# Fixed filters of an image stage on 64x64 tiles of TensorE, with the crossing rows in a packed edge operand

## The chip, the cores and the metric

One core of a Trainium2 chip runs the whole program; the other cores have no work. The metric is the device time of one execution in microseconds (us). The engines are named as in the profile: PE is TensorE's matmuls, PEld its weight loads, DVE is VectorE, ACT is ScalarE, POOL is GpSimd, and SP is SyncE, whose queue issues nearly all DMAs.

## The reference, cut to what matters

The input is `x` of shape (8, 32, 128, 128): images, channels, rows, columns. Four layers follow each other, each adding to `x` a function of the normalised `x`. The change touches the first layer only:

```
x = relu(batchnorm(conv3x3(normalise(x)) + bias))      # y below
grad_x = ifft2(fft2(y) * Fx); grad_y = ifft2(fft2(y) * Fy)          # circular 3x3 Sobel filters
second_xx, second_yy = the same filters again, on grad_x and grad_y
out = second_xx + second_yy + grad_x**2 + grad_y**2 - 2*grad_x*grad_y + y
```

The last line is one linear filter of 5x5 (second_xx + second_yy + y) plus the square of one linear filter of 3x3 (grad_x - grad_y), both circular in rows and columns. All numbers are float32.

## The kernel before, in words

The program has stages, one after the other: the first convolution (to about 260 us), the fixed filters (281 to 731 us, the place of the change), a second layer of small products per pixel (753 to 1680 us), a third and fourth layer (to about 2140 us), and an inverse transform that writes the output.

In the filter stage an image lies with its 128 rows on the 128 partitions and channels and columns along the free axis. A 5x5 circular filter is then five matrix products, one for each column shift `d`: a 128x128 circulant matrix `circ[:, d, :]`, which holds the filter's column along the rows, times the image shifted by `d` columns. The 3x3 filter takes three. A matmul has 512 columns, which is four channels of 128 columns. So an image is 8 groups of four channels, each with `filter5` (L680, five matmuls) and `filter3` (L688, three matmuls). Each float32 matmul shows as two records in the profile. `yp` is the image after batch norm and ReLU, with four wrapped columns in front; ACT makes it from `yt`, a quarter of the channels at a time (`relu`, L960).

`ps` has eight banks. `filter5` of group n writes bank n % 2, `filter3` writes bank 2 + n % 2. ACT squares the second into `sq` (`gradient`, L972). DVE then does for each group (`curvature`, L1367): add the 5x5 result to `xt`, the image of the residual path (L1373, counted by `c5_used`); add the square (L1376, after the semaphore `c3_sq`); take the statistics of the four channels (L1205). `filter5` of group n waits for `c5_used` of group n - 2 and `filter3` for `c3_sq` of group n - 2, so PE works on one bank while the others are read.

The statistics of image h - 1 become its group norm while the filters of image h run: two small products on PE (`group_means`, L627, and `group_vars`, L634), a root on ACT, and scale and shift on DVE (L1225 to L1232). ACT then normalises all 32 channels (L956) into `xn1` in two blocks of 16 instructions, between its work for the groups 1 and 2 and behind group 2, squares them (L982), and DVE sums over channels (L1396) behind the groups 4 and 5. ACT also makes `yp` of image h + 1, a quarter behind each odd group. POOL copies the edge columns (L1166, L1167).

The order of all engines is the order of the code; nothing is reordered by a scheduler. SP's queue does in round h: load the `yt` of image h + 2 (L467), store `xt` of image h - 1 (L472), wait for the normalised image and store it to `xcl` (L477), load `xt` of image h + 1 (L480), in the rounds 1 to 3 issue 36 small DMAs each that place constants of the second layer (`place_tap`, L401 and L403), in round 4 issue 32 loads for the second layer (L446, L455), and store the pixel norms (L498). Each waits its turn behind the ones ahead of it.

## Time and profile before

| what | value |
|---|---|
| median of 3 runs | 2391.45 us (2381.02 to 2391.6) |
| profiled execution, its own time | 2396.21 us |
| its span, first to last instruction | 2394.4 us |
| mean granted clock of TensorE | 0.904 of full speed |
| filter stage, first to last filter matmul | 281.5 to about 731.5 us |
| PE busy in the whole span | 1968.2 us (82%) |
| DVE, ACT, POOL busy | 1210.4, 1137.6, 185.8 us |
| DMA | 306.13 MB, mean 128 GB/s |

### The profile page before, as it was taken

The numbers are of one execution on the slowest core, as the hardware profiler recorded it, in microseconds if no ns is written. First come the engines' busy times: TensorE is split into PE (matmuls) and PEld (weight loads), VectorE is DVE, ScalarE is ACT, GpSimd is POOL, SyncE is SP. The second block draws the span as 40 slices with busy tenths as digits, with TensorE's granted clock in tenths as the row PEclk, the third lists the DMA queues.
The fourth block names the chain that finished last, engine by engine and source line by source line (L and its number), as shares of the span: only waits on it lengthen the run. The fifth ranks groups of instructions, "written<-read, shape, count | busy, mean of one in ns | idle before, by whom it ended". The sixth has DMA issues, their size and how long they took to land.

```text
span 2394.4 us, 85342 instructions
## 1 busy us (share of the span) xinstructions
PE 1968.2 (82%) x38916; PEld 1390.3 (58%) x38916; DVE 1210.4 (51%) x2300; ACT 1137.6 (48%) x1986; POOL 185.8 (8%) x131
## 2 busy tenths in 40 slices
PE   4777599999996989988998999985468888877765
PEld 2344344444444777777777877764465666545654
DVE  3455334444446555555555555541567666722444
ACT  0111336666655555555555555542457766641210
POOL 1000000000010000000000000001333333200000
PEclk9998799999998999999999999997669999976555
DMA  6765844669453444443444344445445452495897
GB/s 136 185 167 124 166 92 101 172 171 230 150 156 114 68 70 81 68 80 67 78 69 78 65 80 71 73 75 172 107 133 155 144 164 85 108 206 167 169 294 221
DMA packets 610284, 306.13 MB, mean 128 GB/s; under 512 B 418236, under 2 KB 586054, under 8 KB 602566
## 3 DMA queue, kind: packets, MB, share of 16 engines
q1 hardware_dynamic: 599376, 283.93, 51.5%
q10 hardware_dynamic: 10560, 16.93, 2.9%
q8 instruction: 295, 4.83, 0.9%
q14 instruction: 53, 0.43, 0.1%
HBM read 172.28 MB, written 128.54 MB: 126 GB/s over the span
## 4 chain that ended last, share of the span: by engine, by line
PE 65%; DVE 9%; ACT 7%; SPq 7%; DMA 7%; issue 5%; ACTq 0%; POOL 0%; DVEq 0%
PE ps L685 12%; PE ps L644 12%; PE ps L764 11%; PE ps L692 7%; PE ps L723 7%; PE ps L748 6%; SPq L455 5%; ACT arena L956 4%; DMA arena<-xcl 4%; PE ps L803 3%; DVE arena L1496 2%; ACT arena L1044 2%; PE ps L918 2%; DMA arena<-x_dram 1%; DVE arena L1418 1%
## 5 line engine op out<-in xcount | busy, mean ns | idle before, releaser
L1418 DVE TENSOR_TENSOR arena<-arena 128x1024 f32<-128x1024 f32 (+1 forms) x308 | 350.7, 1160 | 240.3 <-ACT arena L1036 239.5
L748 PE MATMUL ps<-arena 62*64 62x108 f32 x11008 | 338.6, 257 | 91.8 <-DMA arena<-xcl 59.2
L1036 ACT ACTIVATE arena<-ps 128x1024 f32<-128x1024 f32 (+1 forms) x308 | 297.3, 982 | 150.7 <-PE ps L723 150.4
L748 PEld LDWEIGHTS ps<-arena 62*64 62x64 f32 x11008 | 291.5, 134 | 131.6 <-issue 37.2
L723 PE MATMUL ps<-arena 63*64 63x128 f32 (+1 forms) x9504 | 326.4, 271 | 28.9 <-issue 14.9
L1044 ACT COPY arena<-ps 128x864 f32<-128x864 f32 x258 | 222.4, 880 | 265.7 <-PE ps L764 241.5
L956 ACT ACTIVATE arena<-arena,nmr,rstd 128x128 f32<-128x128 f32 x752 | 295.2, 512 | 31.5 <-DVE nmr L1232 31.5
L723 PEld LDWEIGHTS ps<-arena 63*64 63x64 f32 x9504 | 280.4, 135 | 36.1 <-issue 20.6
L685 PE MATMUL ps<-arena 128*128 128x512 f32 x640 | 289.1, 597 | 14.6 <-ACT arena L970 14.6
L764 PE MATMUL ps<-arena 64*64 64x384 f32 (+1 forms) x3168 | 264.7, 482 | 1.2 <-issue 1.2
L685 PEld LDWEIGHTS ps<-arena 128*128 128x128 f32 x640 | 120.8, 190 | 167.9 <-issue 167.9
L764 PEld LDWEIGHTS ps<-arena 64*64 64x64 f32 x3168 | 149.6, 136 | 91.7 <-issue 26.7
L644 PE MATMUL ps<-arena 32*32 32x512 f32 x4608 | 172.2, 649 | 36.6 <-issue 30.7
L644 PE MATMUL ps<-arena,w_conv 32*32 32x512 f32 x4608 | 176.5, 640 | 12.0 <-DVE arena L1531 6.7
L692 PE MATMUL ps<-arena 128*128 128x512 f32 x384 | 176.3, 594 | 0.0
L644 PEld LDWEIGHTS ps<-arena 32*32 32x32 f32 x4608 | 99.7, 107 | 102.6 <-issue 68.9
L1205 DVE BATCH_NORM_STATS2 st<-arena 128x6 f32<-128x128 f32 x768 | 156.2, 276 | 2.2
L1181 POOL TENSOR_TENSOR arena<-arena 128x1024 f32<-128x1024 f32 x32 | 83.4, 2639 | 937.7 <-DMA arena<-l_dram 937.3
L1431 DVE TENSOR_SCALAR arena<-ps,bias 128x192 f32<-128x192 f32 x172 | 60.0, 411 | 189.0 <-PE ps L764 189.0
L1376 DVE TENSOR_TENSOR arena<-arena 128x512 f32<-128x512 f32 x64 | 47.4, 740 | 160.5 <-ACT arena L975 159.7
L644 PEld LDWEIGHTS ps<-arena,w_conv 32*32 32x32 f32 x4608 | 78.6, 107 | 82.1 <-issue 52.9
L692 PEld LDWEIGHTS ps<-arena 128*128 128x128 f32 x384 | 72.0, 189 | 89.2 <-issue 87.7
(135 smaller groups left out, 1806.1 us busy)
## 6 DMA issues: line engine op xcount, KB each, us to landing
arena<-xcl SPq DMA_DIRECT2D x688, 60.0 KB, 2.7
x_dram<-arena SPq DMA_DIRECT2D x16, 2048.0 KB, 7.1
arena<-x_dram SPq DMA_DIRECT2D x16, 2048.0 KB, 15.1
arena<-l_dram SPq DMA_DIRECT2D x32, 1024.0 KB, 13.5
xcl<-arena SPq DMA_DIRECT2D x8, 3072.0 KB, 10.9
arena<-in_x SPq DMA_DIRECT2D x32, 512.0 KB, 10.5
y_dram<-arena ACTq DMA_DIRECT2D x64, 256.0 KB, 5.7
arena<-in_x SPq DMA_DIRECT2D x16, 1024.0 KB, 16.4
```

What stands on the lines that cost most here:

```text
L455: sp.dma_start(dst, src).then_inc(xs_loaded[e], 16)
L644: m = pe.matmul(ps[C * j:C * j + C, bank + g, :], weights[C * g:C * g + C, dy, dx, :], tile[C * g:C * g + C, r:r + CR, dx:dx + W], start=t ...
L685: m = pe.matmul(ps[:, n % 2, :], circ[:, d, :], yp[h % 2][:, 4 * n:4 * n + 4, 4 - d:4 - d + W], start=d == 0, stop=d == 4)
L692: m = pe.matmul(ps[:, 2 + n % 2, :], circ[:, 5 + d, :], yp[h % 2][:, 4 * n:4 * n + 4, 4 - d:4 - d + W], start=d == 0, stop=d == 2)
L723: mm = pe.matmul(ps[T2 * t:T2 * t + T2, fill_bank(f) + e, i:sub * n:sub], w_op[T2 * e:T2 * e + C + LANES + 1, FILL * f + sub * e + i, :], ...
L748: mm = pe.matmul(ps[T2 * j:T2 * j + T2, bank + t, STEPS * uu:STEPS * uu + STEPS], xs[T2 * t:T2 * t + C + LANES, e, j, u, :], own[T2 * t:T2 ...
L764: mm = pe.matmul(ps[T2 * t:T2 * t + T2, MIX_BANK + j, 0:n // 2 * HALF_U * PIX], w_mix[T2 * j:T2 * j + T2, kk, :], ysb[T2 * j:T2 * j + T2, ...
L956: m = nc.scalar.activation(tile[:, c], src[:, c], ACT.Identity, scale=rstd[:, gn.slot + n % 2, c:c + 1], bias=nmr[:, gn.slot + n % 2, c:c ...
L1036: nc.scalar.activation(own, raw_op, ACT.Tanh).then_inc(fill_tanh, 1)
L1044: nc.scalar.copy(ysb[:, :, e, u:u + UG, :].rearrange("p t u s -> p t (u s)"), ps[:, bank:bank + 2, 0:UG * STEPS]).then_inc(main_out_a, 1)
L1205: m = nc.vector.bn_stats(st[:, c, :], tile[:, c, :])
L1418: nc.vector.tensor_tensor(own, own, d, ALU.add).then_inc(op_done, 1)
```

## The change

Each filter's 128x128 product is cut into products of 64x64. Rows 0 to 63 and rows 64 to 127 of the image are two halves. Only the circulant's diagonal blocks are used, and the rows that cross from one half into the other (four at most) come from a separate operand.

- Each group is now a pair of groups: 8 channels, of which the even ones go to one bank and the odd ones to the next. For odd channels the two halves lie swapped in `yp`, so that the four combinations of row half and output half are four different tiles of the array. A column shift is four matmuls (two banks, two halves), 64 rows by 64 outputs by 512 columns.
- The crossing rows lie in `edge[k]`, for 16 channels each: the last four rows of the other half in five column shifts, 20 partitions for each half. They are copied out of `yp` by ten DMAs of 4 partitions x 2108 elements (`edges_in`). Two copies per image make 20 DMAs. `w_edge` holds the matching filter rows, placed once by 16 small DMAs. Each pair of groups takes four more matmuls for each filter, 20 rows by 64 outputs.
- Semaphores count pairs: `filter5` of pair p starts when `c5_used` shows both banks of the pair before as read, and `filter3` when `c3_sq` does.
- `yt` is gone: `y` is loaded straight into `yp`, which has three buffers, in four DMAs per image in place of two, and ReLU works in place.
- The taps are spread over the rounds 1 to 5 of SP, two each (one in the last), 24 small DMAs in place of 36.

```diff
@@ -55,6 +55,7 @@
+EDGE = C * YPW // 2
@@ -246,13 +247,14 @@
-        xt = [planes(0), planes(22656)]
-        yt = [planes(4096), planes(8192)]
-        yp = [planes(12288, YPW), planes(26752, YPW)]
...
+        xt = [planes(0), planes(22912)]
+        yp = [planes(4096, YPW), planes(8320, YPW), planes(27008, YPW)]
+        edge = [part(12544 + EDGE * n, EDGE).rearrange("p (c w) -> p c w", w=YPW) for n in range(2)]
...
+        w_edge = part(48076, 2 * T2).rearrange("p (a n) -> p a n", a=2)
@@ -432,9 +436,40 @@
-            rows_in(yt[0], image(y_dram, 0), yt_loaded[0])
-            rows_in(yt[1], image(y_dram, 1), yt_loaded[1])
+            def y_in(b):
+                own = yp[b % 3][:, :, YPW - W:YPW].rearrange("p (c s) w -> p c s w", s=2)
+                src = image(y_dram, b).rearrange("h (c s) w -> s h c w", s=2)
+                for s in range(2):
+                    for half in range(2):
+                        rows, at = slice(T2 * half, T2 * half + T2), T2 * ((half + s) % 2)
+                        sp.dma_start(own[rows, :, s], src[s, at:at + T2]).then_inc(y_loaded[b % 3], 16)
+            def edges_in(b, k):
+                sp.wait_ge(relu_done, 4 * b + 2 * k + 2)
+                if b:
+                    sp.wait_ge(c3_mm, 8 * (b - 1) + 4 * k + 4)
+                n = EDGE - 4
+                src = yp[b % 3][:, 16 * k:16 * k + 16, :].rearrange("p c w -> p (c w)")
+                dst = edge[k].rearrange("p c w -> p (c w)")
+                for half in range(2):
+                    last = T2 * (1 - half) + T2 - 4
+                    for d in range(5):
+                        sp.dma_start(dst[T2 * half + 4 * d:T2 * half + 4 * d + 4, 0:n], src[last:last + 4, 4 - d:4 - d + n]).then_inc(edge_loaded[k], 16)
+            y_in(0)
+            y_in(1)
             rows_in(xt[1], image(x, 1), xt_loaded[1])
+            sp.wait_ge(circ_made, 1)
+            sp.wait_ge(edge_clear, 1)
+            for half in range(2):
+                for d in range(8):
+                    at = T2 * half + 4 * (d % 5)
+                    sp.dma_start(w_edge[at:at + 4, d // 5, :], circ[T2 - 4:T2, d, T2:P]).then_inc(edge_made, 16)
+            for part_ in range(2):
+                edges_in(0, part_)
@@ -463,9 +498,12 @@
-                    sp.wait_ge(relu_done, 4 * (h + 1))
-                    rows_in(yt[h % 2], image(y_dram, h + 2), yt_loaded[h % 2])
+                    if h:
+                        sp.wait_ge(c3_mm, 8 * h)
+                    y_in(h + 2)
                 if h == 0:
+                    for part_ in range(2):
+                        edges_in(1, part_)
@@ -476,12 +514,14 @@
+                    edges_in(h + 1, 0)
+                if h + 1 < B:
                     sp.wait_ge(x1_stored[par], 16 * ((h - 1) // 2 + 1))
                     rows_in(xt[par], image(x, h + 1), xt_loaded[par])
-                if h <= 3:
+                if h <= 5:
                     if h == 1:
                         sp.wait_ge(op_taken, 16 * TAPS)
-                    for j in range(3 * (h - 1), 3 * h):
+                    for j in range(2 * (h - 1), min(2 * h, TAPS)):
@@ -496,6 +536,8 @@
+                if h + 1 < B:
+                    edges_in(h + 1, 1)
@@ -677,29 +719,43 @@
-            def filter5(h, n):
-                pe.wait_ge(relu_done, 4 * h + n // 2 + 1)
-                after(pe, c5_used, 8 * h + n - 1)
-                for d in range(5):
-                    m = pe.matmul(ps[:, n % 2, :], circ[:, d, :], yp[h % 2][:, 4 * n:4 * n + 4, 4 - d:4 - d + W], start=d == 0, stop=d == 4)
-                m.then_inc(c5_mm, 1)
-            def filter3(h, n):
-                after(pe, c3_sq, 8 * h + n - 1)
-                for d in range(3):
-                    m = pe.matmul(ps[:, 2 + n % 2, :], circ[:, 5 + d, :], yp[h % 2][:, 4 * n:4 * n + 4, 4 - d:4 - d + W], start=d == 0, stop=d == 2)
-                m.then_inc(c3_mm, 1)
+            def filters(h, p, kernel, first, shifts, bank):
+                for d in range(shifts):
+                    for s in range(2):
+                        for half in range(2):
+                            rows, to = slice(T2 * half, T2 * half + T2), T2 * ((half + s) % 2)
+                            pe.matmul(ps[to:to + T2, bank + s, :], circ[rows, first + d, rows],
+                                      yp[h % 3][rows, 8 * p + s:8 * p + 8:2, 4 - d:4 - d + W], start=d == 0, stop=False)
+                for s in range(2):
+                    for half in range(2):
+                        rows, to = slice(T2 * half, T2 * half + 20), T2 * ((half + s) % 2)
+                        c = 8 * (p % 2)
+                        m = pe.matmul(ps[to:to + T2, bank + s, :], w_edge[rows, kernel, :], edge[p // 2][rows, c + s:c + 8:2, 0:W], start=False, stop=True)
+                return m
+            def filter5(h, p):
+                pe.wait_ge(relu_done, 4 * h + p + 1)
+                if p % 2 == 0:
+                    pe.wait_ge(edge_loaded[p // 2], 160 * (h + 1))
+                after(pe, c5_used, 8 * h + 2 * p)
+                filters(h, p, 0, 0, 5, 0).then_inc(c5_mm, 2)
+            def filter3(h, p):
+                after(pe, c3_sq, 8 * h + 2 * p)
+                filters(h, p, 1, 5, 3, 2).then_inc(c3_mm, 2)
+            pe.wait_ge(edge_made, 16 * 16)
             for h in range(B):
-                for n in range(8):
-                    filter5(h, n)
-                    if n == 1 and h:
+                for p in range(4):
+                    filter5(h, p)
+                    if p == 0 and h:
+                        group_means(gn1, h - 1)
+                    filter3(h, p)
+                    if p == 0 and h:
                         group_vars(gn1, h - 1)
-                    filter3(h, n)
-                    if n == 0 and h:
-                        group_means(gn1, h - 1)
@@ -960,13 +1016,12 @@
-                    act.wait_ge(yt_loaded[h % 2], 32 * (h // 2 + 1))
-                    after(act, c3_mm, 8 * (h - 1))
+                    act.wait_ge(y_loaded[h % 3], 64 * (h // 3 + 1))
                 for c in range(QC * q, QC * q + QC):
-                    m = nc.scalar.activation(yp[h % 2][:, c, 4:YPW], yt[h % 2][:, c, :], ACT.Relu, scale=bn_a[:, c:c + 1], bias=bn_b[:, c:c + 1])
+                    m = nc.scalar.activation(yp[h % 3][:, c, 4:YPW], yp[h % 3][:, c, 4:YPW], ACT.Relu, scale=bn_a[:, c:c + 1], bias=bn_b[:, c:c + 1])
                 m.then_inc(relu_main, 1)
                 act.wait_ge(relu_main, 4 * h + q + 1)
-                tile = yp[h % 2][:, QC * q:QC * q + QC, :]
+                tile = yp[h % 3][:, QC * q:QC * q + QC, :]
@@ -1366,16 +1424,17 @@
-                own = xt[h % 2][:, 4 * n:4 * n + 4, :].rearrange("p c w -> p (c w)")
+                c0 = 8 * (n // 2) + n % 2
+                own = xt[h % 2][:, c0:c0 + 8 - n % 2:2, :]
                 if n == 0:
                     dve.wait_ge(xt_loaded[h % 2], 32 * (h // 2 + 1))
                 dve.wait_ge(c5_mm, 8 * h + n + 1)
-                nc.vector.tensor_tensor(own, own, ps[:, n % 2, :], ALU.add).then_inc(c5_used, 1)
+                nc.vector.tensor_tensor(own, own, ps[:, n % 2, :].rearrange("p (c w) -> p c w", c=4), ALU.add).then_inc(c5_used, 1)
                 dve.wait_ge(c3_sq, 8 * h + n + 1)
                 dve.wait_ge(c5_used, 8 * h + n + 1)
-                nc.vector.tensor_tensor(own, own, sq[:, n % 2, :], ALU.add).then_inc(c3_used, 1)
+                nc.vector.tensor_tensor(own, own, sq[:, n % 2, :].rearrange("p (c w) -> p c w", c=4), ALU.add).then_inc(c3_used, 1)
                 dve.wait_ge(c3_used, 8 * h + n + 1)
-                m = group_stats(xt[h % 2], 4 * n, 4)
+                m = group_stats(xt[h % 2], c0, 4, 2)
```

On PE, at the start of an image's filters, this stood before (L685 `filter5`, L692 `filter3`, L627 and L634 the two norm products; a row without waits follows the one with them):

```order
L627 MATMUL ps<-st,k 128x32 [waits gn1_stats]
L627 MATMUL ps<-st,k 128x32
L685 MATMUL ps<-arena 128x512 [waits c5_used,relu_done]
L685 MATMUL ps<-arena 128x512 x4
L634 MATMUL ps<-dev,k 128x32 [waits gn1_dev]
L634 MATMUL ps<-dev,k 128x32
L692 MATMUL ps<-arena 128x512 [waits c3_sq]
L692 MATMUL ps<-arena 128x512 x2
```

And this stands there now (L728 the shifts of either filter, L734 its edge products, L669 and L676 the two norm products):

```order
L728 MATMUL ps<-arena 64x512 [waits c5_used,edge_loaded0,relu_done]
L728 MATMUL ps<-arena 64x512 x19
L734 MATMUL ps<-arena 64x512 x4
L669 MATMUL ps<-st,k 128x32 [waits gn1_stats]
L669 MATMUL ps<-st,k 128x32
L728 MATMUL ps<-arena 64x512 [waits c3_sq]
L728 MATMUL ps<-arena 64x512 x11
L734 MATMUL ps<-arena 64x512 x4
L676 MATMUL ps<-dev,k 128x32 [waits gn1_dev]
L676 MATMUL ps<-dev,k 128x32
L728 MATMUL ps<-arena 64x512 [waits c5_used,relu_done]
```

Five and three matmuls for four channels became 24 and 16 for eight channels; a wait on `c5_used` now stands once per pair.

On SP, from round 4 into round 5, this stood before (L446 and L455 the second layer's loads, L498 the pixel norms, L360 loads of `y` or `x`, L472 the store of `xt`, L477 the store to `xcl`):

```order
L446 DMA arena<-nimg 30x4x32 x15
L455 DMA arena<-xcl 30x16x32 x16
L498 DMA nimg<-rn 128x192 [waits norm_root]
L360 DMA arena<-y_dram 64x32x128 [waits relu_done]
L360 DMA arena<-y_dram 64x32x128
L472 DMA x_dram<-arena 128x4096 [waits gn1_stats]
L477 DMA xcl<-arena 128x6144 [waits edge_done,gn1_out]
L360 DMA arena<-in_x 64x32x128 [waits x1_stored0]
```

And this stands there now (L460 the edge copies, L447 the loads of `y`, L364 of `x`):

```order
L481 DMA arena<-nimg 30x4x32 x15
L490 DMA arena<-xcl 30x16x32 x16
L538 DMA nimg<-rn 128x192 [waits norm_root]
L460 DMA arena<-arena 4x2108 [waits c3_mm,relu_done]
L460 DMA arena<-arena 4x2108 x9
L447 DMA arena<-y_dram 64x16x128 [waits c3_mm]
L447 DMA arena<-y_dram 64x16x128 x3
L510 DMA x_dram<-arena 128x4096 [waits gn1_stats]
L515 DMA xcl<-arena 128x6144 [waits edge_done,gn1_out]
L460 DMA arena<-arena 4x2108 [waits c3_mm,relu_done]
L460 DMA arena<-arena 4x2108 x9
L364 DMA arena<-in_x 64x32x128 [waits x1_stored0]
```

Ten edge copies stand behind the store to `xcl` and ahead of the load of `xt`, and ten more at the end of the round, behind everything that the round issues.

## Rows read from the trace of the kernel before

**Rows 1.** The chain that ended last, one line of code each: start us, us, what.

```profile
444.65 4.30 PE ps L685 x10
...
451.54 4.30 PE ps L685 x10
...
807.78 5.84 PE ps L764 x72
```

**Rows 2.** By windows: us; busy PE, PEld, DVE, ACT, POOL; clock, DMA share, GB/s.

```profile
458.80:514.80 56.00, 56.00 (x137) 25.02 (x137) 24.22 (x61) 34.61 (x85) 2.43 (x2) 1.00 0.67 171
```

**Rows 3.** Same stretch by lines: engine, op, names, shapes, count, busy us, mean ns, idle.

```profile
L956 ACT ACTIVATE arena<-arena,nmr,rstd 128x128 f32<-128x128 f32 x32 | 12.7, 576 | 0.0
...
L966 ACT ACTIVATE arena<-arena,bn_b,bn_a 128x128 f32<-128x128 f32 x32 | 12.7, 481 | 0.0
...
L1396 DVE TENSOR_REDUCE r<-arena 128x32 f32<-128x1024 f32 x4 | 4.7, 1204 | 0.0
...
L982 ACT ACTIVATE arena<-arena 128x1024 f32<-128x1024 f32 x4 | 4.1, 1052 | 2.9 <-DVE r L1396 2.8
```

**Rows 4.** Timeline of ACT and DVE inside that image: start us, us, line, op, names.

```profile
476.24 0.61 ACT L975 ACTIVATE arena<-ps 128x512 f32<-128x512 f32 x1
...
476.89 0.69 DVE L1376 TENSOR_TENSOR arena<-arena 128x512 f32<-128x512 f32 x1 [5.66 <-ACT arena L975]
...
477.61 0.87 DVE L1205 BATCH_NORM_STATS2 st<-arena 128x6 f32<-128x128 f32 x4
...
478.40 0.67 DVE L1373 TENSOR_TENSOR arena<-arena,ps 128x512 f32<-128x512 f32 x1
```

**Rows 5.** Timeline of DVE where the norm's scale is made.

```profile
463.57 0.19 DVE L1225 TENSOR_SCALAR sd<-ps 128x32 f32<-128x32 f32 x1 [1.26 <-PE ps L634]
...
464.55 0.68 DVE L1373 TENSOR_TENSOR arena<-arena,ps 128x512 f32<-128x512 f32 x1
```

**Rows 6.** Timeline of SP's queue ahead of the filters.

```profile
277.45 10.79 SPq L360 DMA_DIRECT2D arena<-in_x  x2
```

**Rows 7.** Windows over the first filter microseconds.

```profile
287.00:298.00 11.00, 11.00 (x26) 4.79 (x26) 2.94 (x7) 4.89 (x13) 0.00 (x0) 0.99 1.21 203
298.00:320.00 22.00, 22.00 (x52) 9.60 (x51) 7.16 (x19) 8.96 (x22) 0.00 (x0) 1.00 0.52 89
```

**Rows 8.** Timeline of PE at the first filters.

```profile
281.49 7.32 PE L685 MATMUL ps<-arena 128*128 128x512 f32 x10 [14.62 <-ACT arena L970]
```

**Rows 9.** Lines of small DMAs that SP issues: ns min, median, max to issue.

```profile
L424 SPq DMA_DIRECT2D arena<-in_conv_w x16: 427/502/594, 32.3 to 40.6; - x16
...
L401 SPq DMA_DIRECT2D w_dram<-op_dram x81: 712/713/5085, 383.5 to 527.6; - x81
```

**Rows 10.** Timeline of SP's queue in the fifth filter image.

```profile
555.32 12.25 SPq L446 DMA_DIRECT2D arena<-nimg  x16
567.61 8.12 SPq L455 DMA_DIRECT2D arena<-xcl  x16
```

**Rows 11.** Timeline of PE in the first convolution: the bracket is the idle time ahead.

```profile
62.34 4.45 PE L644 MATMUL ps<-arena 32*32 32x512 f32 x128 [1.85 <-issue]
...
132.29 7.03 PE L644 MATMUL ps<-arena 32*32 32x512 f32 x150 [2.84 <-issue]
```

**Rows 12.** Windows there, with the columns of Rows 2.

```profile
60.50:62.30 1.80, 0.00 (x0) 0.00 (x0) 0.57 (x1) 1.19 (x2) 0.00 (x0) 1.00 0.98 295
...
133.90:136.90 3.00, 3.00 (x66) 1.52 (x37) 1.51 (x3) 0.00 (x0) 0.00 (x0) 0.50 0.00 0
```

**Rows 13.** Timeline of PE where two tile shapes alternate.

```profile
1801.77 3.41 PE L644 MATMUL ps<-arena,w_conv 32*32 32x512 f32 x96
1805.10 2.00 PE L803 MATMUL ps<-k,arena 128*128 128x64 f32 x16
1807.03 3.41 PE L644 MATMUL ps<-arena,w_conv 32*32 32x512 f32 x96
```

**Rows 14.** By form: the spectrum's products.

```profile
L885 PE MATMUL ps<-arena 32*64 32x16 f32 x1024 | 30.0, 265 | 17.9 <-issue 15.5 <-ACT arena L1080 2.3
```

21 lines of the change are left out of this document (13 added, 8 removed).

## The prediction

> **What bounds the kernel now.** I read four views in this order. First the chain that ended last, through the filter stage: it is PE alone. A new group of four channels starts every 6.89 us (451.54 - 444.65) [rows 1], and ten records of a group take 4.30 us, 0.43 us each. Eight groups are 55.1 us and the two norm products bring an image to 56.0 us. Then the windows of one image: PE is busy for 56.00 of 56.00 us at clock 1.00, ACT for 34.6, DVE for 24.2, POOL for 2.4, and the DMA engines for 0.67 of the time, which is 37.5 us [rows 2]. So PE is the only full engine, and ACT is the next at 62%. Then the lines of that image, for what ACT and DVE do [rows 3], and the timeline, for how long the hand-over of one group from PE over ACT to DVE lasts [rows 4]. Today that hand-over lies beside PE's next group, since the waits reach back two groups.
>
> **What the change takes from PE.** The price of a 64x64 matmul is in the second layer: 72 records of 384 columns in 5.84 us [rows 1] are 81.1 ns each, so 512 columns should take 81.1 x 512 / 384 = 108 ns. A pair of groups (8 channels) is 24 + 16 = 40 matmuls, 80 records, 8.65 us: 5.2 us for the 5x5 filter and 3.45 us for the 3x3. Two groups of today are 13.77 us. On PE alone an image would fall from 56 to about 35.4 us, and the stage by 8 x 20.6 = 165 us. That is the gain on offer.
>
> The edge products have 20 rows, perhaps another tile shape to the array. The trace has two shapes in turn: 96 records of 32x32 and 16 of 128x128 repeat every 5.26 us (1807.03 - 1801.77) [rows 13]. At 34.8 ns (4.45 us for 128, [rows 11]) the 96 take 3.34 us, and 16 records, 2.00 us by the row with the overlap of their ends, 1.93 us by starts (1807.03 - 1805.10). That leaves nothing for the change of shape. The Trainium skill (TensorEngine Tiling (Array Packing), Key Properties) says that a change of tiling mode drains TensorE; the row shows a drain that costs under 0.1 us. I take nothing; the bound from above is 0.2 us per filter call, 12.8 us in all 64 calls.
>
> **What the pair counting puts on the path.** This is the step on which I rest the forecast. The filter of pair p + 1 now waits until DVE has read both banks of pair p. DVE works in its order: add the 5x5 result of the first bank, wait for ACT's square, add it, take the statistics, and only then add the 5x5 result of the second bank. ACT's square waits for the end of the pair's 3x3 filter. So behind the last matmul of a pair stand, one after the other and with PE empty, the square, the add, the statistics and the next add: from 476.24 to 479.07, 2.83 us [rows 4], and about 0.2 us for three hand-overs between engines. I take 3.0 us for each pair.
>
> In three places more is queued on DVE or ACT in that gap:
> - Pair 0 has the norm's scale between the statistics and the second add: 0.98 us (464.55 - 463.57) [rows 5]. The two norm products are 0.4 us each on PE, and the second lies beside the gap's start: 8.65 + 0.8 + (3.0 + 0.98 - 0.4) = 13.1 us.
> - Pair 1 is 8.65 + 3.0 = 11.7 us. ACT normalises 16 channels beside it.
> - Pair 2 waits for ACT, which from the end of pair 1's filters does a square (0.6), 16 normalisations (half of 12.7), a square, a ReLU quarter (a quarter of 12.7, and its copy, 3.4) and two squares of the norm (half of 4.1) [rows 3]: 13.0 us, against 3.0 + 8.65 = 11.65 of PE, so 1.35 us late. Behind it DVE has the two channel sums, half of 4.7 us [rows 3], ahead of the second add of that pair. So its gap is 3.0 + 1.35 + 2.35 = 6.7 us, and the pair 15.3.
> - Pair 3 is 11.7 us.
>
> An image is 13.1 + 11.7 + 15.3 + 11.7 = 51.8 us in place of 56.0. Of the 20.6 us taken from PE, 16.4 come back as waiting. Image 0 has no norm to make: 4 x 11.7 = 46.8 us.
>
> **What the gaps do to the clock.** Today PE is never idle here and the clock stays at 1.00 [rows 2]. In the first convolution, after 2.84 us of idle PE, 150 records took 7.03 us instead of 150 x 34.8 ns = 5.2 us [rows 11], and the window shows the granted clock at 0.50 (1.2 GHz) for some 3 us [rows 12]. After 1.85 us of idle it stayed at 1.00 [rows 11, 12]. So a gap of about 3 us can bring a spell at 1.2 GHz that costs about 1.7 us; no row tells that it always does. An image has gaps of about 3.6, 3.0, 6.7 and 3.0 us. Bounds: one spell (behind the long gap) and four, 1.7 and 6.8 us per image (none at all is the faster rival). I take three, 5.1 us, nearest to the row with 2.84 us. The image then takes 56.9 us, a little over today's.
>
> **What the start costs.** Ahead of the first filter, SP issues the loads of `y` 0 and 1 and `xt` 1; its issue ends at 288.24 [rows 6], and the DMA engines are full until about 298 [rows 7]. Now 16 copies of filter rows and the ten edge copies of image 0 stand behind them, and the first filter waits for both. A small copy costs 0.50 us to issue [rows 9], so 26 are 13 us: 301.3, and with about 1 us for the last to land (an estimate, the engines being free by then) 302.5. Today the first filter starts at 281.49 [rows 8]. That is +21 us. A bound from below is copies that pass the loads under way and issue at once (+8 us); from above 0.71 us per issue as for the taps [rows 9], +27 us.
>
> **The other costs.** SP per round: 20 edge copies are 10 us, the taps 24 x 0.71 = 17 us [rows 9]. The store to `xcl` is issued about 31 us into an image (pair 0, the filters of pair 1, a square, 16 normalisations and POOL's 2.4 us). Behind it edge copies, `xt`, taps and edge copies are 5 + 7 + 17 + 5 = 34 us, 65 in all, and 66 with the landing. The second batch is needed by pair 2 of the next image, at 56.9 + 13.1 + 11.7 + 3.4 = 85 us: 19 us to spare. Only round 4 has the 32 loads besides, 12.25 + 8.12 us [rows 10], and is 1 to 9 us late once; I take 4. DMA work per image is 37.5 us [rows 2] plus 0.67 MB of copies, at 200 GB/s [rows 7] 3.4 us: it fits beside PE if the copies are spread. `xt` lands about 17 us behind the store, at 50 us, ahead of its use. ReLU in place and the strided adds move the same elements: nothing. The norm chain behind the last image is as before.
>
> **Sum.** First filter at 302.5; image 0 46.8, with 3 us of slow clock at its start (10 records took 7.32 us, not 4.30 [rows 8], which today's number holds too) and 4 us for spells; seven images of 56.9 are 398.3; 4 us for round 4; less the last hand-over, 3 us. That ends at 755.6, against 731.5 today: +24 us. The profiled execution took 2396.21 us, 4.8 over the median of the runs shown, 2391.45; on the median the forecast is 2415 us. About 0.5% (12 us) is what a measurement of this kernel can tell from no change.
>
> **Rivals.**
> - The clock holds through 3 us gaps, and only the gap behind pair 2 costs a spell. Images are 53.5 us, the end is at 729: 2389 us, no change. For it: no row has gaps of 3 us that recur with 8.7 us of dense work between. Against it: rows 11.
> - The clock holds and the start costs only +8 us, or the hand-over is shorter than 3 us. With no spell at all the stage ends at 717 - 13 = 704: 2364 us, faster. For it: the copies move little, and each 1 us off the hand-over gives 31 us. Against it: rows 4 and 11.
> - Two row halves cannot write one bank at a time, although to different partitions. Then two tiles run at once and not four: 216 ns per record, a pair 17.3 us of filters, an image 4 x 17.3 + 0.8 + 3.6 + 3.0 + 5.35 + 3.0 = 85 us, and the kernel some 245 us slower, 2636 us. In today's second layer each row half has a bank of its own; only the spectrum's products have two row groups on one bank, 29.3 ns each with 16 columns [rows 14], too short to decide but without a stall.
> - The edge copies are slow because four partitions keep only a few of the 16 DMA engines busy. An engine moves 203 GB/s / 16 = 12.7 GB/s [rows 7] and has 37.5 us of other work in an image, so 56.9 - 37.5 = 19 us are left for 0.67 MB of copies: it decides from fewer than three engines. On four, an image's copies take 13 us of each and are hidden; on two, 26.5, and an image takes 64 us, the kernel some 50 us more than the forecast, 2465 us. For it: the shape of 4 rows. Against it: no row shows a copy that uses few engines.
>
> The Trainium skill (TensorEngine Tiling (Array Packing), Gotcha 1: PSUM Pressure) states the rule behind the third rival: different row tiles cannot access the same PSUM bank simultaneously. No run here shows it with long matmuls.
>
> **Chances.** Forecast 0.58, clock holds 0.18, faster case 0.10, one bank 0.06, slow copies 0.08. The forecast's own range is 2398 (two spells, or a start of +13) to 2440 (four spells and 0.2 us per filter call). The range of 8 in 10 takes in the unchanged case and reaches up toward the slow copies: 2380 to 2462. Slower by over 0.5%: most of the forecast, 0.52, and the last two, 0.14, so 0.66. Within 0.5%: the rest of the forecast 0.06, and 0.16 of the clock case, 0.22. Faster: 0.12.
>
> **What would show it.** The start: first filter at 302 us in the timeline of PE. The pair: the filter records at about 108 ns each by busy time, and an idle gap of PE in front of each pair's first matmul, put down to DVE's L1432, the 5x5 add, of 2.5 to 3.5 us, and one over 6 us ahead of pair 3. Busy PE in the stage about 60 to 70% at a clock near 0.8 in the windows. If the gaps are under 2 us, the step on pair counting is wrong. If they are there and the clock is 1.00, the clock step is. If PE waits for a DMA ahead of the pairs 0 or 2 in most images, the SP step is.

## The result and the profile after

The changed kernel takes 2503.12 us (median of 4 runs, 2502.62 to 2511.52) against 2389.6 us (4 runs, 2381.02 to 2391.6) for the kernel before on the same chip. The ratio is 1.0487, with a 95% interval of 1.0459 to 1.0515. The forecast was 2415 us with a range up to 2462: the sign is right, the size is not.

The profiled execution took 2502.77 us, its span is 2501.0. The filter stage runs from 317.96 to 847.7 us, 530 us in place of 450. What stands behind the stage takes 1653 us, against 1663 before; over all runs below it is 1651 to 1667 without any pattern. So everything is decided up to the end of the filter stage, and I compare kernels by the start of each image. The first filter itself moves between profiles of kernels that leave the start alone (314.9 to 326.6 us), so the length of the stage says more than its end.

TensorE's waits in the stage (what waits, line, releaser: us in total, times, longest):

```profile
PE ps L728 <- DMA arena<-arena: 121.3, 9, 51.0
PE ps L728 <- DVE arena L1432: 88.3, 23, 5.3
```

L728 is the 64x64 filter. Its releaser `DMA arena<-arena` is an edge copy, the only transfer from SBUF to SBUF; DVE's L1432 is the 5x5 add. The second row was forecast. The first was forecast for the start only. A whole image of the timeline of PE (start us, us; the bracket is the idle time ahead, here as in [rows 8]):

```profile
503.09 6.14 PE L728 MATMUL ps<-arena 64*64 64x512 f32 x40 [3.45 <-DMA arena<-arena]
509.16 1.09 PE L734 MATMUL ps<-arena 20*64 20x512 f32 x8
...
518.58 6.92 PE L728 MATMUL ps<-arena 64*64 64x512 f32 x40 [3.44 <-DVE arena L1432]
525.43 1.09 PE L734 MATMUL ps<-arena 20*64 20x512 f32 x8
526.45 2.81 PE L728 MATMUL ps<-arena 64*64 64x512 f32 x24
529.19 1.09 PE L734 MATMUL ps<-arena 20*64 20x512 f32 x8
540.03 6.44 PE L728 MATMUL ps<-arena 64*64 64x512 f32 x40 [9.75 <-DMA arena<-arena]
...
556.53 6.72 PE L728 MATMUL ps<-arena 64*64 64x512 f32 x40 [5.29 <-DVE arena L1432]
...
571.90 3.29 PE L728 MATMUL ps<-arena 64*64 64x512 f32 x16 [3.88 <-DMA arena<-arena]
```

Four pairs, each behind a gap. The third stands behind 9.75 us and not 3.03, because its half of the edge operand has not arrived. The 24 records of the 3x3 filter take 2.74 us from start to start (529.19 - 526.45), 114 ns each; the 40 of the 5x5 filter behind a gap take 6.1 to 6.9 us. The same view without a gap ahead, in a later variant, has 4.53 us for them.

By windows (columns as in [rows 2]), an image without and one with a late copy:

```profile
373.90:434.50 60.60, 45.85 (x328) 14.45 (x329) 24.17 (x62) 35.45 (x85) 2.42 (x2) 0.84 0.60 149
503.10:571.90 68.80, 46.45 (x328) 14.27 (x329) 24.69 (x63) 35.05 (x87) 2.43 (x2) 0.80 0.64 149
```

Against [rows 2] PE falls from 56.00 busy of 56.00 to 46 of 60.6 or 68.8, and the clock from 1.00 to 0.84 and 0.80. DMA still shows a share of 0.64, so the DMA engines as a whole are not full. Image starts are 318.0, 373.9, 434.5, 503.1, 571.9, 641.3, 726.1, 789.2: periods of 55.9, 60.6, 68.6, 68.8, 69.4, 84.8, 63.1, 58.5 us.

The hand-over in image 1, timeline of all engines, to be read against [rows 4]:

```profile
399.61 1.09 PE L734 MATMUL ps<-arena 20*64 20x512 f32 x8
400.76 0.60 ACT L1030 ACTIVATE arena<-ps 128x512 f32<-128x512 f32 x1 [2.91 <-PE ps L734]
...
401.39 0.69 DVE L1435 TENSOR_TENSOR arena<-arena 128x512 f32<-128x512 f32 x1 [3.70 <-ACT arena L1030]
402.12 0.87 DVE L1260 BATCH_NORM_STATS2 st<-arena 128x6 f32<-128x128 f32 x4
402.91 0.67 DVE L1432 TENSOR_TENSOR arena<-arena,ps 128x512 f32<-128x512 f32 x1
403.73 2.64 PE L728 MATMUL ps<-arena 64*64 64x512 f32 x12 [3.03 <-DVE arena L1432]
```

Square, add, statistics, second bank's add, and only then PE: 3.03 us, step by step as forecast.

SyncE's queue (start us, us held, line), at the start and around image 2:

```profile
281.35 7.78 SPq L364 DMA_DIRECT2D arena<-in_x  x2
289.23 14.50 SPq L470 DMA_DIRECT2D arena<-arena  x16
303.77 20.84 SPq L460 DMA_DIRECT2D arena<-arena  x20
```

```profile
456.81 10.32 SPq L460 DMA_DIRECT2D arena<-arena  x10
467.19 6.81 SPq L447 DMA_DIRECT2D arena<-y_dram  x4
...
477.62 6.45 SPq L460 DMA_DIRECT2D arena<-arena  x10
486.96 16.02 SPq L364 DMA_DIRECT2D arena<-in_x  x2
503.03 6.27 SPq L405 DMA_DIRECT2D w_dram<-op_dram  x3
```

Sixteen filter rows took 0.91 us each and edge copies 1.04 us each, not 0.50. A round of SyncE (456.8 to 525.5) is 68.7 us, the period of the image. While ten edge copies were most of the traffic the window shows:

```profile
457.00:467.00 10.00, 4.91 (x44) 1.23 (x40) 2.84 (x7) 6.86 (x18) 0.00 (x0) 0.92 0.26 36
```

0.26 of 16 engines is 4.1 engines at work, at 36 GB/s together. Of these 0.36 MB a store of 96 KB, issued just before (`nimg<-rn`), is 0.1 MB, so the copies alone run at 26 GB/s, 6.5 GB/s for each of four engines. The whole image before had 171 / (0.67 x 16) = 16 GB/s per busy engine [rows 2]. Ten copies are 0.33 MB, 12.9 us at this rate: SyncE is let go after 10.3 us, and the pair that waits for them starts at 471.26, 4.1 us behind that.

### The profile page after: what moved, and what is told of

Read it like the earlier page. It is cut to its first block, busy times and chain, and to the rows that moved or that the text cites. A ratio compares the mean times of both kernels' runs of the same rounds, so it can differ in the third digit from the quotient of the medians.

```text
span 2501.0 us, 88586 instructions
## 1 busy us (share of the span) xinstructions
PE 1874.0 (75%) x40452; PEld 1305.9 (52%) x40452; DVE 1208.0 (48%) x2302; ACT 1136.9 (45%) x1986; POOL 185.9 (7%) x131
## 4 chain that ended last, share of the span: by engine, by line
PE 49%; SPq 19%; DVE 10%; DMA 8%; ACT 7%; issue 5%; ACTq 0%; POOL 0%; DVEq 0%
PE ps L686 11%; PE ps L820 10%; PE ps L779 6%; PE ps L804 6%; SPq L490 5%; PE ps L728 5%; ACT arena L1012 4%; DMA arena<-xcl 4%; SPq L364 3%; SPq L460 3%; SPq L405 3%; PE ps L859 3%; SPq L447 2%; DVE arena L1555 2%; DMA x_dram<-arena 2%
## 5 line engine op out<-in xcount | busy, mean ns | idle before, releaser
L728 PE MATMUL ps<-arena 64*64 64x512 f32 x2048 | 300.3, 735 | 209.7 <-DMA arena<-arena 121.3
L728 PEld LDWEIGHTS ps<-arena 64*64 64x64 f32 x2048 | 94.3, 165 | 401.8 <-issue 401.5
L820 PEld LDWEIGHTS ps<-arena 64*64 64x64 f32 x3168 | 157.3, 134 | 82.6 <-issue 14.4
L1030 ACT ACTIVATE arena<-ps 128x512 f32<-128x512 f32 x64 | 37.6, 594 | 276.8 <-PE ps L734 276.8
L1432 DVE TENSOR_TENSOR arena<-arena,ps 128x512 f32<-128x512 f32 x64 | 43.5, 680 | 187.2 <-PE ps L734 185.2
```

Of the source, the lines that this page charges most:

```text
L728: pe.matmul(ps[to:to + T2, bank + s, :], circ[rows, first + d, rows], yp[h % 3][rows, 8 * p + s:8 * p + 8:2, 4 - d:4 - d + W], start=d == ...
L820: mm = pe.matmul(ps[T2 * t:T2 * t + T2, MIX_BANK + j, 0:n // 2 * HALF_U * PIX], w_mix[T2 * j:T2 * j + T2, kk, :], ysb[T2 * j:T2 * j + T2, ...
```

## The experiments

Three theories. **H**: the hand-over behind each pair of banks, and the clock it costs, is everything. **Q**: SyncE's queue is full by its number of issues. **D**: each edge copy is slow on its few DMA engines, and holds up whatever comes behind it. Times are medians; the ratio is to the kernel before on the same chip, whose median was 2393 to 2396 us in all of them. Image periods are the differences of image starts in the timeline of PE.

**taps_early.** The nine taps of the next layer's operator go from SyncE's rounds 1 to 5 to ScalarE's queue during the first convolution; the edges stay.

```
-                if h <= 5: ...  place_tap(j)        # SyncE
+                    if 0 <= j < TAPS:               # ScalarE, behind y of image b
+                        place_tap(j)
```

> The changed kernel, with the 108 small tap DMAs issued on ACT's queue during the first convolution and none on SP in the filter stage. Theory Q (SP's queue, issuing and being held up by full DMA queues, sets the 69 us rounds of the images 2 to 5): the rounds lose about 22 us of SP time, fall below PE's own 60.6 us, and the stage ends about 45 us earlier, 2455 us; PE's waits for edge copies fall from 121 us (51 of them ahead of the first filter) to under 75. Rival H (the hand-over at each pair, with its clock, sets the images): nothing on SP matters, 2500 us. Rival D (four partitions keep the copies on few DMA engines and these are full): the taps move 0.03 MB, so no change, 2500 us.

Measured: 2498.78 us, ratio 1.0419 (1.0387 to 1.0451). The first filter came 26 us later, at 344.4, but images 1 to 4 took 60.8 to 61.4 us, with no late copy, and the stage 490 us in place of 530. The 40 us off the stage are near the 45 that Q asked for; the time fell by only 4 us since the taps on ScalarE delayed the start. H and D, in the form that they had here, said that nothing would change, and the images contradict both: the taps are a part of SyncE's round, and without them the copies arrive in time, slow or not. Only image 5 still waits for one, 8.83 us.

**adds_first.** VectorE adds the 5x5 results of both banks as soon as they are there.

```
-                dve.wait_ge(c5_mm, 8 * h + n + 1)
-                nc.vector.tensor_tensor(own, own, ps[:, n % 2, :]...).then_inc(c5_used, 1)
+                for m2 in (n, n + 1) if n % 2 == 0 else ():
+                    dve.wait_ge(c5_mm, 8 * h + m2 + 1)
+                    nc.vector.tensor_tensor(own1, own1, ps[:, m2 % 2, :]...).then_inc(c5_used, 1)
```

> The changed kernel, with DVE adding both banks' 5x5 results of a pair before it waits for the first square; all else as it was. The gap of 3 us behind each pair should go for every theory, if it is what the rows say. Theory Q: only images that don't wait for SP gain (0, 1, 6, 7), 12 to 18 us each, and the gain comes out at 30 to 60 us, 2455 us; the images 2 to 5 keep 68 to 70 us and PE's waits for edge copies grow. Rival H: all eight images gain 18 us, 144 us in all, 2360 us.

Measured: 2466.31 us, ratio 1.0292 (1.0255 to 1.0328). Only 37 us, where H asked for four times that. The 3 us gaps are gone, and waits for edge copies stand in their place; PE's waits in the stage:

```profile
PE ps L728 <- DMA arena<-arena: 105.6, 7, 50.4
PE ps L728 <- issue: 83.8, 6, 30.3
```

The profile puts the second row on no releaser, but it stands ahead of pair 2 in the images 2 to 7 and is the same wait: in image 2 the copies' issue ends at 452.21 and the pair starts at 456.44, 4.2 us later. Image 0 took 39.5 us, but images 2 to 4 70.6, 68.7 and 69.1, as slow as before the edit: H alone falls. Images 0, 1, 6 and 7 gained 7 to 16 us each, as Q had it.

**one_copy_of_five.** The five shifted copies of four rows are one DMA, so 4 issues an image and not 20; bytes, source and row length are the same.

```
-                    for d in range(5):
-                        sp.dma_start(dst[... 4 rows ...], src[last:last + 4, 4 - d:4 - d + n])
+                    wide = bass.AP(tensor=own.tensor, offset=own.offset, ap=[list(own.ap[0]), [1, 5], [1, n]])
+                    sp.dma_start(to, wide)
```

> The changed kernel, with the five shifted copies of a half in one DMA (20 partitions x 2108 elements out of 4 rows), 4 edge DMAs per image for 20; the same bytes, and the rows of the packed operand in another order. Theory Q: SP loses 16 issues of 0.6 to 1.0 us in a round, which falls from 69 to about 56 us, under PE's 60.6; with round 4 still long, some 40 to 45 us are gained, 2460 us. Rival D: the same bytes over the same engines, no change, 2500 us. Rival H: no change but for the start (about 8 us).

Measured: 2506.74 us, ratio 1.0466 (1.0436 to 1.0497), images 2 to 4 still at 65 to 68 us. The issues themselves fell to 1.4 to 3.1 us a batch, but the y loads behind them were then held 13.7 to 15.6 us instead of 6.5. The number of issues is not the cause: Q falls in this form.

**edges_before_x.** At the start the filter rows and image 0's edge copies go ahead of the second y and x loads.

> The changed kernel, with the 16 copies of filter rows issued behind the load of y 0 and the edge copies of image 0 ahead of the load of xt 1. All theories: only the start moves. The first filter comes at about 309 us for 318, since 7.8 us of issue no longer stand ahead; the gain is 8 to 10 us, 2493 us.

Measured: 2498.37 us, ratio 1.0414 (1.0376 to 1.0452). First filter at 306.1, 11.8 us sooner; stage end 835.9, 11.9 us sooner, since images 2 to 5 still took 69 to 85 us. In the medians 5 us, not told from scatter.

**no_edge_copies.** Edge copies left out from image 1 on.

```
             def edges_in(b, k):
+                if b:
+                    return
```

> The edge copies are left out from the second image on (TensorE multiplies what image 0 left in the packed operand, so the four seam rows of images 1 to 7 are not computed from their own data); the multiplies and all else stay. All theories but H: images take what TensorE's own path asks, 56 to 61 us as images 0 and 1 of the kernel after did, the stage that began at 318 us ends near 318 + 8 x 59 = 790 instead of 848, and the time is 2440 to 2455. If images still take over 65 us, the copies are not what holds TensorE and the bound is in SyncE's taps and x loads (no difference from 2503 above 15 us). If images fall to 52 us (my forecast's sum of row halves and hand-overs without a clock penalty beyond it), the copies also cost the clock, and the time is near 2395.

Measured: 2467.51 us, ratio 1.0309 (1.0265 to 1.0354). PE's waits in the stage:

```profile
PE ps L730 <- DVE arena L1434: 112.5, 31, 5.3
PE ps L730 <- DMA arena<-arena: 51.5, 1, 51.5
```

Every image from 2 to 6 took 61.3 to 61.4 us: gaps of 3.03, 3.44, 3.03 and 5.28 us and nothing else. That is the price of hand-over and clock together; the stage, from 326.6 to 807.7, takes 481 us, and the copies cost the other 49 us. In the medians the difference is 36 us, since the first filter came 8.6 us later here and what stands behind the stage took 3 us more.

**edges_on_pool** and **edges_on_act.** The 20 copies of an image are issued by GpSimd, or by ScalarE behind the second and fourth normalised quarter.

```
-                        sp.dma_start(dst[...], src[...]).then_inc(edge_loaded[k], 16)
+                        pool.dma_start(...)     # or act.dma_start(...)
```

> The edge copies (all 20 of an image, same bytes, same order) are issued by GpSimd instead of SyncE, ahead of its work on the image before; nothing else changes. In the profile after, the copies move alone at 25 to 57 GB/s with a DMA share near 0.2 of 16 engines, and ten of them take about 10 us. Theory D (backlog on the few DMA engines that serve copies issued from SyncE: each copy has four partitions): what decides is which engines carry them. If copies from GpSimd's queue are dealt over more than those four, ten of them land within about 3 us of each other, the nine waits of TensorE for edge copies (121 us, 51 of them at the start) fall under 60 us, images 3 to 5 take 60 to 62 us instead of 68.6, and the time falls by 30 to 50 us, to 2453 to 2475. Theory S (SyncE's queue itself, 68.7 us always busy in a round): the same fall, since 20.8 us of a round leave SyncE. Theory H (the hand-over after each pair of banks is all there is): no change, 2495 to 2510. D and S are told apart by the next kernel, which moves the copies to ScalarE's queue. Price against both: GpSimd's own work on the image before (its reorder into the next layer's form) waits behind 20 issues; if an issue costs it over 1 us, SyncE waits for GpSimd over 20 us per round and the gain halves.

> The 20 edge copies of an image are issued by ScalarE, ten behind the second and ten behind the fourth normalised quarter of the next image; SyncE issues none. Same partitions and bytes. Theory S (SyncE's queue is what is full): SyncE's round falls from 68.7 to about 48 us, the waits for edge copies fall to those of the start, images take 60 to 62 us, 2455 to 2475. Theory D (four DMA engines are behind; ScalarE's queue deals copies of four partitions to engines as SyncE's does): the waits stay at 9 to 10 us in an image whose x and y loads stand ahead of the copies, they shrink only by what SyncE no longer holds up, so images of 64 to 68 us and 2480 to 2503. Both have a price in ScalarE: 20 issues of some 0.6 us are 12 us per image beside its 32 us of work, so the first pair of each image may start 1 to 3 us later.

Measured: on GpSimd 2490.89 us, ratio 1.0417 (1.0376 to 1.0458), images 2 to 5 at 63 us; on ScalarE 2545.24 us, ratio 1.0631 (1.0588 to 1.0675), images at 74 to 76 us. GpSimd missed the expected fall by 16 us and more; its image 6 kept a wait of 26.6 us at the second pair. ScalarE came out slower than either theory had it, since neither counted that the hold-up would move with the copies. The queues, ScalarE's first:

```profile
452.29 10.97 ACTq L1047 DMA_DIRECT2D arena<-arena  x10
...
488.93 15.84 ACTq L1047 DMA_DIRECT2D arena<-arena  x10
```

```profile
470.40 5.10 POOL L1209 DMA_DIRECT2D arena<-arena  x10 [1.55 <-ACT arena L1005]
```

Ten copies hold ScalarE for 10 to 16 us as they held SyncE, and its square for the pair waits behind them: the hold-up comes with the copies, not with SyncE's load. GpSimd issues ten in 5.1 us.

**pool_all.** edges_on_pool, adds_first and edges_before_x together.

> Three edits together: the edge copies issued by GpSimd, both 5x5 additions of a pair of banks ahead of the 3x3 work on VectorE, and the edge filters and image 0's edge copies ahead of the second x and y loads at the start. D and S: the additions gave 35 us while the copies still cost 10 us per image; with both gone an image is 8.85 x 4 + about 12 us of other work at a higher clock, 48 to 52 us, the stage of eight images is 400 to 420 us from a start at 306 to 310, ends at 710 to 730 and the time is 2365 to 2400, the same as before or up to 1% below. H (hand-over only): 2466 as the additions alone gave, less 12 for the start, 2454. If GpSimd's issues take over 1 us each, its order of work sets the round and the time stays above 2420.

Measured: 2428.09 us, ratio 1.0132 (1.0082 to 1.0181), above the forecast of 2365 to 2400. Images 2 to 4 took 61.4 to 63.3 us, and SyncE shows why:

```profile
486.88 4.26 SPq L494 DMA_DIRECT2D x_dram<-arena  x1
491.64 0.33 SPq L499 DMA_DIRECT2D xcl<-arena  x1
501.40 15.12 SPq L364 DMA_DIRECT2D arena<-in_x  x2
516.57 10.24 SPq L405 DMA_DIRECT2D w_dram<-op_dram  x3
```

It waits 9.4 us for the stored x, is held 15 us by the x load, and 26 us by two taps. With the hand-over gone this chain is the next bound.

**copies_of_16_rows.** The decisive one: same number, bytes, queue and places, other shape (wrong data in the seam rows from image 1 on).

```
+                            c, r0, r1 = n // 4, T2 * half + 16 * (d // 4), T2 * (1 - half) + T2 - 16
+                            sp.dma_start(dst[r0:r0 + 16, c * (d % 4):c * (d % 4) + c], src[r1:r1 + 16, ...])
```

> From image 1 on each edge copy moves 16 partitions of a quarter of the width instead of 4 partitions of the full width: as many copies, from the same queue at the same places, with the same bytes (the multiplies of the seam rows then read wrong data; image 0 keeps its own copies). Theory D (a copy is carried by as many DMA engines as its partitions let it be dealt to, four of them for four rows, and those are behind): ten copies no longer hold SyncE 10.4 us as in the kernel after but 5 to 7, which is what issuing ten of them costs; the waits of TensorE for edge copies after the start go, images 2 to 5 take 61.3 us as they did without any copies, and the time is 2460 to 2475. Theory E (the copies are slow for what they are: rows of SBUF to rows of SBUF, or their number, whatever the engines): ten copies still hold SyncE about 10 us, images 2 to 4 take 68.6 us and the time is 2495 to 2510. Theory Q (SyncE is full by its issues): as E, since the number of issues is unchanged.

Measured: 2470.57 us, ratio 1.0312 (1.0282 to 1.0342), the time of no_edge_copies. Images 2 to 4 took 61.3 to 61.4 us; one copy was late, by 9.06 us in round 4. The two batches and the x load behind the second:

```profile
511.08 6.75 SPq L462 DMA_DIRECT2D arena<-arena  x10
...
537.41 10.00 SPq L462 DMA_DIRECT2D arena<-arena  x10
547.45 2.62 SPq L364 DMA_DIRECT2D arena<-in_x  x2
```

6.75 us against 10.32 for the first batch, and 12.62 against 22.47 for the second and the x load together; without any copies, in no_edge_copies, that x load alone holds SyncE 9.57 us. The stage takes 489 us against 530: the shape of the copy, four rows of 8.2 KB, costs 41 of the 49 us, and most of the rest is the one late copy. The edit changes rows and row length together, so by itself it doesn't tell "few engines" from "long rows". The window over the first batch, to be read against that of 457 to 467 us above:

```profile
511.00:518.00 7.00, 3.55 (x20) 1.46 (x23) 4.37 (x14) 5.21 (x14) 0.00 (x0) 0.66 0.25 58
```

As many engines are busy on the mean (0.25 and 0.26), and they move 58 GB/s, not 36; each window has a store of 96 KB in it, and the copies' own part is 39 and 26 GB/s. So the number of busy engines is not what differs. The traces' records of single packets say what does. In the kernel after each row of a copy is one packet of 8432 bytes, never more than four of them are under way, and the median takes 1.29 us. Where few other packets run beside them, in edges_on_pool, such packets take 319 ns with one under way, 620 with two and 918 with three. That is 26 GB/s in all, whether one engine works on the four rows or four do, so more engines on them would gain nothing. In one_copy_of_five the destination has 20 partitions and the median is again 1.29 us, which points to the four source rows. In copies_of_16_rows the packets have 2108 bytes, up to 16 are under way, and the median takes 125 ns, 17 GB/s for each; the quickest take 85 ns, 25 GB/s, the rate of a long packet alone, so the length of the rows matters little. So D is right that the copies are slow, and wrong that the engines are what they lack.

**adds_no_copies.** adds_first and no_edge_copies together.

> Both 5x5 additions of a pair of banks first on VectorE, and the edge copies left out from image 1 on (the seam rows of images 1 to 7 are then not computed from their own data). What is left is TensorE's own path. D: the two costs that the runs so far show are taken away together; the last image of adds_first, which waited for copies only 5.4 us, took 43.2. Images then take 40 to 46 us, where SyncE allows it: SyncE's round without copies is 46 to 50 us in rounds with taps, so images 2 to 5 take 48 to 56 and the round with the next layer's loads 75; the stage is 400 to 430 us and the time 2375 to 2410. If images take over 60 us, the edge copies cost nothing by themselves in adds_first and the x and y loads or the taps were its bound.

Measured: 2363.12 us, ratio 0.9864 (0.9834 to 0.9895), images 47 to 49.5 us where the taps are. That is under the expected 2375 to 2410. It is what the new tiling gave with its two costs taken away and nothing else moved, 31 us less than the kernel before, in a kernel that leaves the seam rows of images 1 to 7 out. Where no gap stands ahead the clock stays up:

```profile
346.79 4.53 PE L730 MATMUL ps<-arena 64*64 64x512 f32 x40
351.25 1.09 PE L736 MATMUL ps<-arena 20*64 20x512 f32 x8
```

**taps_spread** and **taps_on_pool.** pool_all, with at most two taps in any of SyncE's rounds 1 to 7 (nine in all), or all taps issued by GpSimd.

```
+            TAPS_AT = {1: (0, 1), 2: (2, 3), 3: (4,), 4: (), 5: (5, 6), 6: (7,), 7: (8,), 8: ()}
```

> As pool_all (edge copies by GpSimd, additions first, edge filters early), and the nine taps of the next layer's operator are placed in SyncE's rounds 1 to 7, two, two, one, none, two, one, one, instead of two a round in rounds 1 to 5. In pool_all SyncE's round was 61.5 us: 15 us until the stored image had landed, 15 us of x load, 26 us of two taps, 5 us of y loads. If that chain is the bound (theory S now, for this version), a round with one tap takes 48 to 50 us, round 4 loses 26 of its 91 us, and the time falls from 2428 by 40 to 60 us, to 2370 to 2390, 0 to 1% below the kernel before. If the copies on GpSimd's queue are the bound instead, it stays within 10 us of 2428.

> As pool_all, with the nine taps issued by GpSimd (two, two, and then one behind its work on each image) and none by SyncE. Theory S for this version: SyncE's round falls to 36 us and TensorE's path of 43 to 46 us bounds the images, the stage takes 370 to 390 us and the time is 2320 to 2350, 2 to 3% below the kernel before. The price is GpSimd's: 12 issues a tap, at 0.51 us as its edge copies took 6 us; if small pieces cost it 2 us each, a tap takes 24 us there, the edge copies queued behind it come late by that, and images take 60 us or more (2420 or above).

Measured: 2405.03 us, ratio 1.0036 (1.0016 to 1.0057), and 2408.85 us, ratio 1.0075 (1.0048 to 1.0101). They missed the expected ranges by 15 and 59 us. Image 6, which in pool_all took 91 us behind round 4 of SyncE, fell to 58, but images 1 to 6 stayed at 55 to 65, with waits of 8 to 17 us for copies at the first pair of images 2 to 7, even where SyncE had no taps. A new cause was needed: ScalarE releases those copies late, behind its other work, when the 2 and 3 MB stores are under way.

**relu_early** and **relu_early_taps_pool.** ScalarE normalises the first two quarters of the next image ahead of its work on this one, in taps_spread and in taps_on_pool; GpSimd issues the copies of that half one turn of its loop earlier.

```
+                if h + 1 < B:
+                    relu(h + 1, 0)
+                    relu(h + 1, 1)
                 for n in range(8):
```

> As taps_spread (2405), with ScalarE's normalised quarters 0 and 1 of the next image moved ahead of its work on this image (it idles there 17.9 us), so that GpSimd issues the copies for the next image's first half in the middle of this image, 13 us earlier and ahead of the two stores (5 MB) of the image before. R (late release): the wait of about 10 us for copies at the first pair of images 2 to 7 falls to 0 to 3 us, images take 48 to 52 us, SyncE's rounds of one tap being 48 to 50, the stage ends near 690 and the time is 2340 to 2365, 1 to 2% below the kernel before. E (the copies stay the bound wherever they start): the wait stays at 8 us or more and the time at 2395 to 2410.

> The same move in taps_on_pool (2409), where SyncE places no taps. R: waits for copies at the first pair fall from 11 to 17 us to 0 to 4; SyncE's round is 36 us, so TensorE's path (39.5 us without waits, 44 to 48 with those for ScalarE) bounds the images, and the time is 2320 to 2350. S (SyncE's round): no faster than relu_early by more than 5 us only if SyncE doesn't bound that one. E: 2395 to 2410.

Measured: 2409.08 us, ratio 1.0074 (1.005 to 1.0098), and 2384.97 us, ratio 0.9973 (0.9946 to 1.0). The waits for copies went (to 1.33 us at the first pair in the second version, from 11 to 17), as R says; but both times lie above R's ranges, since PE now waited 8 to 27 us at the second pair for VectorE, and that for the x load of its image. Late release was a true wait with another one just behind it.

**x_load_first** and **x_load_first_taps_sp.** In relu_early_taps_pool and in relu_early, the x load goes ahead of the 3 MB store.

```
+                    rows_in(xt[par], image(x, h + 1), xt_loaded[par])
                 sp.dma_start(image_rows(xcl, h - 1, XROW), ...).then_inc(xn1_stored[par], 16)
-                    rows_in(xt[par], image(x, h + 1), xt_loaded[par])
```

> As relu_early_taps_pool (2385), with the load of x for the image after next's buffer issued ahead of the 3 MB store of the same round. Theory R2 (what is left is the x load behind that store): its landing, 26.3 us after its issue in the profile before this edit, comes 7 to 10 us earlier, the waits at the second pair (13.8, 11.7, 7.9, 20.7, 9.9 us) fall to 2 to 8 us, images take 48 to 52 us and the time is 2345 to 2365, 1 to 2% below the kernel before. Theory B (the DMA engines' total traffic of a round, some 10 MB at 175 GB/s, is the bound whatever its order): images stay at 56 to 60 us and the time within 8 us of 2385.

> The same exchange in relu_early (2409), where SyncE places the taps. R2: the load is issued no earlier than before (SyncE waits 11 us for the x store to land either way) but lands 7 to 10 us earlier, images of 58 to 60 us become 50 to 53 and the time 2365 to 2385. B: 2400 to 2415. If SyncE's own round of issues (61 us with one or two taps) bounds it, as in pool_all, it also stays at 2400 to 2415 while the first run gains.

Measured: 2356.43 us, ratio 0.9842 (0.9814 to 0.987), and 2389.98 us, ratio 0.997 (0.9946 to 0.9993). DMA issues from 380 to 650 us (count, KB each, median us to landing), relu_early_taps_pool and then x_load_first:

```profile
arena<-in_x SPq DMA_DIRECT2D x9, 1024.0 KB, 24.6
```

```profile
arena<-in_x SPq DMA_DIRECT2D x10, 1024.0 KB, 14.7
```

Ten microseconds sooner, images 2 to 4 at 42 to 51 us, and the time 28 us lower: R2 is right for this version. The other, with SyncE's taps, gained 19 us but missed R2's range by 5; three of its images still took 61 to 70 us, with PE waiting 15 to 24 us for VectorE at the second pair. x_load_first computes the whole output and beats both kernels, the one before by 1.6%. Its image 6 still takes 72.8 us, with a wait of 26.4. Whether the kernel before would gain from the same x load order and taps was not tried; its PE is busy without a gap in the image read [rows 2].

## Why the prediction was wrong

The stage end was forecast at 755.6 us and came at 847.7, 92 us later; less the 10 us by which the rest was shorter this is the difference of the profiled execution from its forecast (2502.77 against 2396.21 + 24). By parts: start 15 us (317.96 - 302.5), hand-over and clock 28 (481 of no_edge_copies against 453.1), edge copies 49 (529.7 - 481). The 453.1 hold 4 us for a late round 4; put with the copies, these make the parts 32 and 45.

- **Gain on PE: right, a little small.** 111 to 114 ns a record, 127 ns for the edge products (1.02 us for 8), not 108 for all. A pair is 9.24 us, not 8.65, and an image with its norm products 38.1, not 35.4. If the slower edge products are the change of shape, it costs about 0.1 us per filter call, 1 us an image; nothing was taken for it, with a bound of 0.2.
- **Pair counting: right.** Gaps of 3.03, 3.44, 3.03 and 5.28 us, 14.8 an image where 16.4 were forecast. The step on which I rested the forecast held.
- **Clock: right in kind, too small.** Three spells of 1.7 us were taken. The four 5x5 runs behind the gaps of the image shown take 26.2 us instead of 4 x 4.53, 8.1 us more: a spell that costs 1.6 to 2.4 us behind each gap. With 38.1 and 14.8 that is 61.0, close to the 61.4 of no_edge_copies, against 56.9 forecast.
- **Start: too small.** First filter at 317.96, not 302.5. The working priced 26 small copies at 0.50 us; the filter rows took 0.91 us and the edge copies 1.04, 12 us of the 15. Even the bound of 0.71 us was under both. Another 3 us are the landing, about 1 us by an estimate that no row showed: image 0's first ten copies were issued by about 314.2, 3.8 us ahead of the filter.
- **The step that failed** is the one on the other costs: "DMA work per image is 37.5 us [rows 2] plus 0.67 MB of copies, at 200 GB/s [rows 7] 3.4 us: it fits beside PE if the copies are spread", with the copies landed 66 us into an image and 19 to spare. The rate was wrong by a factor of nearly eight: four rows of SBUF gave 26 GB/s, so the 0.67 MB take 26 us and not 3.4, and they hold up what stands behind them. In the round shown they held SyncE 16.8 us where 10 were counted, and the x load behind them 16 us where 7 were (9.6 without any copies), so that SyncE's round, 68.7 us, is longer than PE's 61.4 and sets the pace. Leaving the copies out took 49 us off the stage. The sign that the forecast named for this, a DMA wait ahead of pair 0 or 2 in most images, is in the timeline, in five of eight images.
- **The rival on slow copies** saw that few engines would carry them and priced it too low: at 12.7 GB/s for an engine, four engines would still hide them. Four rows gave 26 GB/s together, what it expected of two engines. By its own sum that is 26.5 us of copies beside 37.5 of other work, 64 us an image and 2465 us. Images 2 to 4 took 68.6 to 69.4 us, and the copies cost 49 us where it had some 50. So its size came out, with the reason changed: four engines were at work and together did what two were to do. The time still came 38 us above its 2465, since hand-over, clock and start were short too.
- **One bank: refuted.** 216 ns a record were its sign, and 114 were measured with two row halves writing one bank in different partitions. The rule of the Trainium skill (TensorEngine Tiling (Array Packing), Gotcha 1: PSUM Pressure) does not hold for this form.
- **Clock holds, faster case:** refuted by the clock of 0.84 and 0.80 in the windows; a faster kernel needed the gaps taken away, as adds_no_copies shows.

## What to carry to other kernels

Price a small copy by its shape, not its bytes: count the partitions that it reads, and where no row of the trace shows that shape, bound its rate from below before calling it hidden. Where an operand pair is released by the last reader of both halves, let that reader take both halves first; here it took the 3 us gaps away, and behind each of them the slow clock had cost 1.3 us or more again. When a cover is removed, look for the second wait just behind it: here it took four (hand-over, copies, their release, the x load behind a store) until the gain of the tiling appeared, with the taps and the start moved besides.

## What the runs showed of the hardware

- Copies of four rows of 8.2 KB from SBUF to SBUF ran at 26 GB/s in all, whether one packet was under way (319 ns for 8432 bytes) or four (1.29 us each); the same bytes as 16 rows of 2.1 KB ran at 17 GB/s for each packet with up to 16 under way.
- Ten four-row copies held the issuing queue 6.3 to 16.2 us on SyncE and 10 to 16 us on ScalarE, and 5.1 us on GpSimd, 0.51 us for each at whatever load was seen. That the hold is much the same on the first two was not expected.
- Making five copies one gained nothing: the hold moved to the next DMA in the queue.
- Two 64-row halves writing one PSUM bank in different partitions ran at full rate, 114 ns per 512 columns.
- In the 17 profiles of changed kernels, each of the 309 whole 5x5 runs behind a gap of 2.8 us or more took 5.85 to 7.52 us, and without a gap all took 4.53. Behind gaps of 1.33 us both occur: in x_load_first 4.53 us in image 2 and 6.22 in image 3.
